# One Trainium2 core, a fused four-layer sequence kernel: a new planner for the order of work in the causal attention stage

## The chip, the core and the metric

The kernel runs on one core of a Trainium2 chip. A core has five engines, each with an instruction queue of its own that is worked off strictly in order: TensorE (PE in the rows; PEld is its weight load), VectorE (DVE), ScalarE (ACT), GpSimd (POOL) and SyncE (SP), which here only issues DMA transfers. They wait for each other through semaphores alone. The metric is the device time of one execution in microseconds (us), a median over runs. TensorE's clock has two levels, 2.4 GHz and 1.2 GHz; the profile gives what was granted as a share of the upper one.

## The reference

Four residual blocks on an input of 4 batches x 1024 rows x 128 features, each behind a layer norm: window attention, gated linear attention, causal attention with a linear recurrence beside it, and a mixture of experts. The change is in the third, which is, cut to what matters:

```python
q, k, v = split_heads(x @ Wqkv_w + Wqkv_b)            # 16 heads of 8
scores = einsum('bhid,bhjd->bhij', q, k) * scale
y_softmax = softmax(scores + causal_mask) @ v
def step(state, inp):                                  # one step per row of the sequence
    q_t, k_t, v_t = inp
    state = retention * state + Gamma * v_t[..., :, None] * (k_t * scale)[..., None, :]
    return state, einsum('bhij,bhj->bhi', W_static + state, q_t)
alpha = sigmoid(gelu(x @ gate_w1 + gate_b1) @ gate_w2 + gate_b2)
y = alpha * y_softmax + (1 - alpha) * y_stp
return y @ out_w + out_b
```

## The kernel before

The causal stage works on 16 units: 4 batches times 4 groups of 4 heads. For each unit it scores twice. The first time (items `M`, 20 to a unit) PE scores 128 query rows against the keys (L1300, with the mask in L1304 and L1307), and DVE takes the negated maximum of each row (L1450, by 512, 768 or 1024 columns). When the maxima of a unit are complete, DVE joins two halves (L1454), POOL splits them into three bf16 parts (L1698 to L1704), PE turns them (item `S`, L1314), ACT copies them out (L1537), and SP moves them into the query stack by four transfers (L1626). The second time (items `W`, 20 to a unit) PE scores keys against queries with the maxima in the stack (L1329, mask L1333 and L1336), ACT takes the exponential into one of four buffers (L1550), and PE weighs the values (items `V`, 12 to a unit, L1357) into an accumulator that ACT copies out (item `A`, L1556). All of `M`, `S`, `W` and the projections and turns below write PE's output into a ring of three PSUM slots of 1024 columns; a slot may be written again when the engine that reads it is through.

Beside the units stands other work. The next batch is prepared: norm (`stats`, `root`, `turn`), the projections `q` and `k` (PE L948, ACT L997 and a bf16 copy L1002; POOL subtracts it, L1669; item `mid` is ACT's second bf16 part, L1006, with POOL's third behind it, L1675; item `write` is SP's transfers of the three parts to a DRAM scratch, L1029; `L` loads them back into the stacks of the batch, L1616, and the batch's first `M` waits for it), and the gate (`gate1`: PE L1260, ACT L1509 between two table loads; `gate2`, `alpha`). ACT's copy L1002 for `k` overwrites the parts of `q`, and so waits until all of `q`'s are in the scratch. The linear recurrence is row work in 8 rounds a batch: `kv` (POOL L1711), `scan` (DVE L1460), `scale` (ACT L1563), `read` (POOL L1723 and L1726, in the first round L1720), and at its end `less` (POOL L1736, 1 minus alpha), `beta` (PE turns it, L1274; ACT L1527 copies it out), `gated` (POOL L1743). A finished batch is turned and projected (`att`: L1368, L1467, L1470, L1479; `tp`: L1376, L1384, L1386, L1488).

`causal_order` writes one list of all items. Every engine's program walks this list and issues its own part of each item, so the list sets each engine's queue. Before the change, the list comes from fixed rules: a `V` stands one key step late, the beside-work stands at hand-given steps (`prepare`, `finish`, 6 steps to a recurrence round), the turned maxima `S` stand behind the second `M` of the next unit, and `M` is put in ahead of `W` by a lead and by a rough estimate of three engines (`TIMES`, `put`, `begin`). The slot of the n-th ring item is n modulo 3:

```python
                    slot[item] = ring[len(slot) % 3]
                    if ps is not None:
                        if len(taken) >= 3:
                            pe_wait_free(taken[-3])
                        taken.append(item)
```

## Time and profile before

| | |
|---|---|
| runs | median 1811.09 us of 3 (1809.95 to 1813.37) |
| the profiled execution | 1810.67 us, its span 1809.4 us |
| causal stage | from 940 to about 1570 us of the span |
| busy in the whole span | PE 1568.5, DVE 1285.6, ACT 1101.3, POOL 698.2 us |
| granted clock, mean | 0.957 |

The median of the runs is 0.42 us above the profiled execution. The sum is made against 1810.67 us. An engine's busy time is what its instructions took; idle time in front of an instruction is put down to the event that ended it. A matmul's end is modelled, so PE's busy time is an upper reading.

### The profile page before, as it was taken

What the parts mean: (1) busy time and instruction counts of PE and PEld (TensorE: products, weight loads), DVE (VectorE), ACT (ScalarE), POOL (GpSimd) and SP (SyncE); (2) the same over time, 40 slices, a digit from 0 to 9 for tenths busy, and PEclk for the clock granted to TensorE, in tenths of its full rate; (3) what the DMA queues carried; (4) which work ended last, traced back from release to release, by engine and by line L of the source; (5) the groups of instructions that cost most, each with busy time, mean ns of one, the idle gap of its engine ahead of it and who ended that gap; (6) DMA issues with size and microseconds to landing.
All of it is one profiled execution on the core that took longest, in us unless ns stands there. A gap on an engine that the chain in (4) does not pass through costs nothing. (4 is left out here: it accounts for less than half of the span.)

```text
span 1809.4 us, 45598 instructions
## 1 busy us (share of the span) xinstructions
PE 1568.5 (87%) x19728; PEld 1003.6 (55%) x19728; DVE 1285.6 (71%) x2035; ACT 1101.3 (61%) x1642; POOL 698.2 (39%) x500
## 2 busy tenths in 40 slices
PE   4577998999999999999977778878888888899999
PEld 2354666778777778777853323433433332566665
DVE  4665745876787687777768768778778886766564
ACT  3265667777777777786733577677677678433321
POOL 4112301544354255425531555556465555301100
PEclk8798998999999999999996989999999999999999
DMA  7864200000000000000142462164236222000000
GB/s 180 198 181 109 41 5 12 2 2 2 1 2 2 2 2 2 2 2 2 48 110 62 146 155 72 48 187 95 71 116 143 72 71 72 1 7 12 7 12 12
DMA packets 43357, 102.59 MB, mean 57 GB/s; under 512 B 3944, under 2 KB 12288, under 8 KB 41428
## 3 DMA queue, kind: packets, MB, share of 16 engines
q1 hardware_dynamic: 40244, 94.17, 20.2%
q10 hardware_dynamic: 2912, 5.51, 1.8%
q8 instruction: 155, 2.54, 0.6%
q14 instruction: 46, 0.38, 0.1%
HBM read 67.42 MB, written 31.46 MB: 55 GB/s over the span
## 5 line engine op out<-in xcount | busy, mean ns | idle before, releaser
L1450 DVE TENSOR_REDUCE arena<-ring 128x2 f32<-128x1024 f32 (+2 forms) x320 | 342.1, 1111 | 88.8 <-PE ring L1307 63.4
L1550 ACT ACTIVATE arena<-ring 128x1024 f32<-128x1024 f32 (+1 forms) x320 | 291.6, 938 | 129.2 <-PE ring L1336 90.2
L1357 PE MATMUL accs<-arena 128*9 128x512 f32 (+3 forms) x1536 | 174.3, 528 | 2.7 <-ACT arena L1550 2.6
L2514 POOL TENSOR_TENSOR arena<-arena 128x1280 f32<-128x1280 f32 x28 | 65.3, 2332 | 287.0 <-PE accs L2275 231.7
L1329 PE MATMUL ring<-arena 51*128 51x512 bf16 (+3 forms) x768 | 124.4, 342 | 46.6 <-DVE arena L1450 24.9
L1300 PE MATMUL ring<-arena 48*128 48x512 bf16 (+3 forms) x768 | 126.6, 342 | 41.9 <-DVE arena L1450 21.7
L2506 POOL TENSOR_TENSOR arena<-arena 128x512 f32<-128x512 f32 x112 | 141.4, 1292 | 3.0 <-DVE arena L2316 3.0
L292 POOL TENSOR_SCALAR xn<-x,moments,rstd 128x128 f32<-128x128 f32 x80 | 64.4, 814 | 198.2 <-DVE rstd L263 182.6
L2781 ACT ACTIVATE arena<-ring 128x512 f32<-128x512 f32 x80 | 47.8, 598 | 147.2 <-PE ring L2636 142.6
L2499 POOL TENSOR_TENSOR arena<-arena 128x1024 f32<-128x1024 f32 x32 | 86.2, 2694 | 108.2 <-DVE arena L2373 108.2
L2741 DVE TENSOR_TENSOR arena<-arena,ring 128x512 f32<-128x512 f32 x80 | 55.0, 688 | 87.8 <-PE ring L2638 74.2
L1723 POOL TENSOR_TENSOR arena<-arena 128x1024 f32<-128x1024 f32 x28 | 65.9, 2355 | 126.6 <-ACT arena L1563 102.5
L1329 PEld LDWEIGHTS ring<-arena 51*128 51x128 bf16 x768 | 36.5, 95 | 140.3 <-DVE arena L1450 78.0
L2658 PEld LDWEIGHTS accs<-weights_large,arena 128*128 128x128 f32 x640 | 83.5, 191 | 27.1 <-issue 23.5
L1300 PEld LDWEIGHTS ring<-arena 48*128 48x128 bf16 x768 | 37.9, 95 | 108.5 <-DVE arena L1450 41.7
L2658 PE MATMUL accs<-weights_large,arena 128*128 128x128 f32 x640 | 84.5, 275 | 0.5 <-DVE arena L2746 0.5
L2459 ACT ACTIVATE arena<-arena 128x512 f32<-128x512 f32 x128 | 81.6, 709 | 0.0
L633 DVE TENSOR_REDUCE arena<-ring 128x8 f32<-128x1024 f32 x49 | 59.3, 1220 | 25.1 <-PE ring L526 25.0
L2251 PE MATMUL ring<-arena 128*64 128x256 f32 x512 | 76.0, 380 | 0.0
L1711 POOL TENSOR_TENSOR arena<-arena 128x1024 f32<-128x1024 f32 x32 | 75.6, 2361 | 0.1
L1460 DVE TENSOR_TENSOR_SCAN arena<-arena 128x1024 f32<-128x1024 f32 x32 | 73.8, 2307 | 2.4 <-POOL arena L1711 2.3
L2316 DVE SCALAR_TENSOR_TENSOR arena<-ring,arena 128x512 f32<-128x512 f32 x32 | 22.1, 692 | 66.6 <-PE ring L2199 66.6
(346 smaller groups left out, 4225.8 us busy)
## 6 DMA issues: line engine op xcount, KB each, us to landing
arena<-whole_k SPq DMA_DIRECT2D x32, 512.0 KB, 4.6
arena<-whole_q SPq DMA_DIRECT2D x32, 512.0 KB, 6.2
arena<-c_scratch_q SPq DMA_DIRECT2D x14, 384.0 KB, 10.2
arena<-c_scratch_k SPq DMA_DIRECT2D x14, 384.0 KB, 13.3
a_scratch_k<-arena SPq DMA_DIRECT2D x8, 512.0 KB
c_scratch_k<-arena SPq DMA_DIRECT2D x8, 512.0 KB, 3.8
arena<-a_scratch_q SPq DMA_DIRECT2D x9, 384.0 KB, 7.2
arena<-a_scratch_k SPq DMA_DIRECT2D x9, 384.0 KB, 9.5
```

The lines of the kernel that those rows point to most:

```text
L1300: mm = nc.tensor.matmul(o[r], qs[half(r, SCORE), pair, n * P:(n + 1) * P], ks[half(r, SCORE), pair, a:c], start=True, stop=not diag)
L1329: mm = nc.tensor.matmul(o[r], ks[half(r, SHIFT), 2 * g + pair, j * P:(j + 1) * P], qs[half(r, SHIFT), 2 * g + pair, a:a + cols], start=Tru ...
L1357: mm = nc.tensor.matmul(acc[ci % 2][32 * h:32 * h + HD + 1, a - c * BANK:BANK], c_values[b % 2][:, j, r * HEADS // 2 + 2 * g + i, :], weig ...
L1450: nc.vector.tensor_reduce(dst, src, AX.X, ALU.max, negate=True).then_inc(c_max_taken.up(item), 1)
L1460: nc.vector.tensor_tensor_scan(sk[:, :], c_retain[:, j:j + 1].to_broadcast([P, T]), sk[:, :], 0.0, ALU.mult, ALU.add).then_inc(c_state_mad ...
L1550: nc.scalar.activation(view(c_probs[wi % 4]), view(ps), ACT.Exp).then_inc(c_weights_made.up(item), 1)
L1711: nc.gpsimd.tensor_tensor(sk[:, :], sk[:, :], c_vT[:, :], ALU.mult).then_inc(c_kv_made.up((b, j)), 1)
L2251: mm = nc.tensor.matmul(ps[r * GLA_D:(r + 1) * GLA_D, o + GLA_D:o + DENSE * GLA_D], k_nat[1][:, cols], v5[t % 2][:, 1:DENSE, cols], start= ...
L2459: nc.scalar.activation(v5[t % 2][:, 1 + r, :], v5[t % 2][:, 0, :], ACT.Copy, scale=route_hot[t // NT % 2][:, t % NT, r:r + 1]).then_inc(v_ ...
L2499: nc.gpsimd.tensor_tensor(masked[0][:, :], masked[0][:, :], masked[1][:, :], ALU.add).then_inc(gla_joined.up(t), 1)
L2506: nc.gpsimd.tensor_tensor(pair_cols(q2m[:, r, :]), pair_cols(q2[t % 2][:, :]), hot_b[t % 2][:, r * P:(r + 1) * P].unsqueeze(1).to_broadcas ...
L2658: mm = nc.tensor.matmul(moe_total[:, n * P:(n + 1) * P], hid[i % 3][:, n * P:(n + 1) * P], w("d_down", f * P, (f + 1) * P), start=f == 0 a ...
```

## The change

`causal_order` gets a new estimate of four engines (PE `P`, ACT `A`, DVE `D`, POOL `G`) with other durations (`STEP`, `NEXT`, `LATER`), a function `ready` that says when an item's data are made by this estimate, and a greedy choice: of `W`, `V`, `S`, `M` and the beside-work on PE, the one that the estimate starts first, with a bonus or malus each. Beside-work without a part on PE goes in where its data are ready by the estimate or three key steps after its due step. `S` is put where the maxima are estimated ready. `less` and the recurrence are two queues, with `after` keeping the order that the data need. A ring item takes the slot that the estimate frees first, and waits for the item that held this slot. The number and kind of instructions stay the same. The core of the diff:

```diff
-            HOP = 0.2
-            TIMES = {"turn": (1.1, (("A", 0.6),), 1), "q": (2.0, (("A", 1.1),), 1), "k": (2.0, (("A", 1.1),), 1),
...
+            HOP, SWITCH = 0.06, 0.2
+            STEP = {"turn": (0.65, ["A", 0.6]), "q": (1.95, ["A", 1.1]), "k": (1.95, ["A", 1.1]), "v": (0.95, ["D", 0.7]),
...
+            LATER = {"root": ["G", 3.3], "turn": ["G", 5.8], "q": ["A", 1.1, "G", 2.2], "k": ["A", 1.1, "G", 2.2],
+                     "mid": ["G", 2.6]}
...
+            def ready(item):
+                kind = item[0]
+                at = lambda *names: max([made.get(n, 0.0) for n in names])
+                if kind == "V":
+                    return at(("W", *item[1:], len(score_pairs(*item[3:5])) - 1))
+                if kind == "W":
+                    return at(("S", *item[1:3], part_of(*item[1:4]))) + (2.2 if item[4:] == (0, 0) else 0.0)
+                if kind == "S":
+                    return at(("neg", *item[1:4]))
...
+                before = {"log": ("stats", b, 3), "root": ("log", b), "gate1": ("turn", b, 1), "gate2": ("gate1", b),
+                          "gate exp": ("gate2", b), "alpha": ("gate exp", b), "less": ("alpha", b), "beta": ("less", b),
+                          "v": ("turn", b, 1), "q": ("turn", b, 1)}
...
+                if kind == "k":
+                    return at(("mid", b, "q", "end")) + 5.0
...
+                return at(before[kind]) if kind in before else 0.0
...
+                if on_ring:
+                    place_of[item] = free.index(min(free))
+                    free[place_of[item]] = done
...
+            def delay(item):
+                pe_time, drain = pe_and_drain(item)
+                behind = clock[drain[0]] - begin(item) - pe_time if drain else 0.0
+                return begin(item) + 0.5 * max(0.0, behind)
+
+            while weights or values or turned:
+                for queue in sides:
+                    while due(queue) and may_go(queue):
+                        put(queue.pop(0)[1])
+                choices = []
+                if weights and not (values and step_of[weights[0][:5]] >= step_of["W", *values[0][1:]] + 2):
+                    if ("S", *weights[0][1:3], part_of(*weights[0][1:4])) in made:
+                        choices.append((delay(weights[0]), "W"))
+                if values and (not weights or step_of[weights[0][:5]] > step_of["W", *values[0][1:]]):
+                    choices.append((begin(values[0]) + (0.25 if weights else 0.0), "V"))
+                if turned and not second:
+                    choices.append((begin(turned[0]) - 0.3, "S"))
...
+                    loaded = not b or ("L", b, "k", g // 2 * 2, g // 2 * 2 + 2) in made
+                    if loaded and taken < (done + most) * ratio and not (turned and last):
+                        choices.append((delay(ahead[0]) - (1.0 if taken < (done + lead) * ratio else 0.0), "M"))
+                if due(sides[0]) and pe_and_drain(sides[0][0][1])[0]:
+                    choices.append((delay(sides[0][0][1]) - 0.2 * (at - sides[0][0][0]), "side"))
+                kind = min(choices)[1]
...
-                    slot[item] = ring[len(slot) % 3]
+                    k = place_of[item] if item in place_of else last_used.index(min(last_used))
+                    slot[item], held_before[item] = ring[k], last_used[k][1]
+                    last_used[k] = len(slot) + 2, item
...
-                    if ps is not None:
-                        if len(taken) >= 3:
-                            pe_wait_free(taken[-3])
-                        taken.append(item)
+                    if held_before.get(item):
+                        pe_wait_free(held_before[item])
```

For an `M` of a later batch the new list asks that its load `L` stands ahead of it (`loaded`); `ready` gives such an `M` no time of its own.

What this moves is shown at three places. Lines are those of each kernel; the new code shifts them by 94 in this stage, so that L1550 becomes L1644, and by 1 in the helpers, so that L997 becomes L998.

ACT, where `k` of the last batch is prepared. Before:

```order
L997 ACTIVATE arena<-ring,arena 128x1024
L1002 ACTIVATE arena<-arena 128x1024
L1563 ACTIVATE arena<-arena,weights_small 128x1024
L1537 ACTIVATE arena<-ring 12x1024
L1550 ACTIVATE arena<-ring 128x1024 x2
L1509 ACT_TABLE_LOAD
L1509 ACTIVATE arena<-ring,weights_small 64x1024
L1511 ACT_TABLE_LOAD
L1550 ACTIVATE arena<-ring 128x1024 x2
L1006 ACTIVATE arena<-arena 128x1024
```

And of the change, with the exponentials ahead of it:

```order
L1007 ACTIVATE arena<-arena 128x1024
L1631 ACTIVATE arena<-ring 12x1024
L1644 ACTIVATE arena<-ring 128x1024 x4
L998 ACTIVATE arena<-ring,arena 128x1024
L1003 ACTIVATE arena<-arena 128x1024
L1605 ACT_TABLE_LOAD
L1007 ACTIVATE arena<-arena 128x1024
L1644 ACTIVATE arena<-ring 128x2x384 x2
```

Between `k`'s first copy and its second part (`mid`) there were four exponentials, a scale and an `S`, and now there is only the gate. The second parts of `q` and `k` are both later in the list. Counted over the list, `k` of batches 1, 2 and 3 stood behind 30, 110 and 190 items `W` and now stands behind 36, 117 and 196; the first `M` of these batches stood behind 46, 126 and 206 and now stands behind 45, 129 and 203. Between `k` and that `M` there were 16 `W` and 20 or 21 `M` each time; now there are 9, 12 and 7 `W` and 12, 12 and 8 `M`.

POOL, the end of the recurrence of the last batch. Before (L1711 is `kv`, L1736 is `less`, L1743 is `gated`):

```order
L1726 TENSOR_TENSOR arena<-arena 128x1024
L1711 TENSOR_TENSOR arena<-arena 128x1024
L1736 TENSOR_SCALAR arena<-arena 128x1024
L1723 TENSOR_TENSOR arena<-arena 128x1024
L1726 TENSOR_TENSOR arena<-arena 128x1024
L1743 TENSOR_TENSOR arena<-arena 128x1024
```

And of the change, where they are L1805, L1830 and L1837:

```order
L1830 TENSOR_SCALAR arena<-arena 128x1024
L1817 TENSOR_TENSOR arena<-arena 128x1024
L1820 TENSOR_TENSOR arena<-arena 128x1024
L1805 TENSOR_TENSOR arena<-arena 128x1024
L1817 TENSOR_TENSOR arena<-arena 128x1024
L1820 TENSOR_TENSOR arena<-arena 128x1024
L1837 TENSOR_TENSOR arena<-arena 128x1024
```

`less` has moved ahead of a `read` (two instructions) and a `kv`; it stands so in all four batches.

PE, at the start of unit (batch 1, group 1), with the slots' numbers. Before:

```order
L1300 MATMUL ring1<-arena 128x512 x2
L1329 MATMUL ring2<-arena 128x512 x2
L1333 MATMUL ring2<-bf_causal_col,bf_half_rows 128x64 x2
L1336 MATMUL ring2<-bf_causal_col,bf_half_rows 128x128 x2
L1300 MATMUL ring0<-arena 128x256 x2
L1304 MATMUL ring0<-bf_causal_row,bf_half_rows 128x128 x2
...
L1329 MATMUL ring1<-arena 128x512 x2
L1333 MATMUL ring1<-bf_causal_col,bf_half_rows 128x64 x2
L1336 MATMUL ring1<-bf_causal_col,bf_half_rows 128x128 x2
L1357 MATMUL accs<-arena 9x128 x4
```

And of the change:

```order
L1451 MATMUL accs<-arena 9x256 x4
L1423 MATMUL ring2<-arena 128x512 x2
L1427 MATMUL ring2<-bf_causal_col,bf_half_rows 128x64 x2
L1430 MATMUL ring2<-bf_causal_col,bf_half_rows 128x128 x2
L1451 MATMUL accs<-arena 9x128 x4
L1423 MATMUL ring1<-arena 128x512 x2
L1427 MATMUL ring1<-bf_causal_col,bf_half_rows 128x64 x2
L1430 MATMUL ring1<-bf_causal_col,bf_half_rows 128x128 x2
L1394 MATMUL ring0<-arena 128x512 x2
L1394 MATMUL ring2<-arena 128x512 x2
L1451 MATMUL accs<-arena 9x512 x4
```

The second `W` of the unit took the slot of the third ring item before it; now it takes that of the second before it. Of the 819 ring items with a holder, 702 keep a distance of three in the new list, 60 have two, 50 have four, and 7 another; alternations of `M` and `W` are about as many as before (an `M` takes a slot from a `W` 158 times before and 155 times now).

## Rows read from the trace of the kernel before

**Rows 1.** Busy time by stretch: us, engines (instructions), granted clock, DMA share, GB/s.

```profile
935.00:1108.00 173.00, 130.44 (x1430) 54.74 (x1430) 134.19 (x147) 94.19 (x109) 73.14 (x57) 0.86 0.50 123
1108.00:1258.00 150.00, 124.42 (x1450) 53.31 (x1448) 117.18 (x133) 103.01 (x121) 83.19 (x54) 0.95 0.42 107
```

**Rows 2.** PE's waits, 940 to 1570 us: in total, times, longest.

```profile
PE ring L1329 <- DVE arena L1450: 24.9, 51, 1.2
PE ring L1300 <- DVE arena L1450: 21.7, 36, 3.1
PE ring L1300 <- ACT arena L1550: 11.6, 29, 1.4
PE ring L1329 <- ACT arena L1537: 9.4, 3, 6.0
PE ring L1314 <- POOL arena L1704: 9.1, 7, 2.1
PE ring L1274 <- POOL arena L1736: 6.7, 4, 3.6
PE ring L1329 <- ACT arena L1550: 5.7, 14, 0.8
```

**Rows 3.** Timeline, 1034 to 1045 us: start, duration, instruction, idle time before it.

```profile
1041.16 1.06 ACT L1002 ACTIVATE arena<-arena 128x1024 bf16<-128x1024 f32 x1 [3.80 <-DMA c_scratch_q<-arena]
...
1044.32 0.61 PE L1329 MATMUL ring<-arena 51*128 51x512 bf16 x2 [6.05 <-ACT arena L1537]
```

**Rows 4.** Timeline at the last batch's `beta`.

```profile
1545.27 1.97 PE L1274 MATMUL ring<-weights_constants,arena 128*128 128x128 f32 x8 [3.60 <-POOL arena L1736]
```

**Rows 5.** Groups by shape, 940 to 1570 us: busy, mean ns, idle before.

```profile
L1450 DVE TENSOR_REDUCE arena<-ring 128x2 f32<-128x1024 f32 x192 | 228.3, 1218 | 52.7 <-PE ring L1307 28.1 <-PE ring L1300 23.4
L1550 ACT ACTIVATE arena<-ring 128x1024 f32<-128x1024 f32 x224 | 222.7, 1023 | 97.9 <-PE ring L1336 60.3 <-PE ring L1329 37.3
L1550 ACT ACTIVATE arena<-ring 128x768 f32<-128x768 f32 x64 | 51.3, 813 | 17.2 <-PE ring L1336 16.2
L1563 ACT ACTIVATE arena<-arena,weights_small 128x1024 f32<-128x1024 f32 x32 | 39.6, 1237 | 5.9 <-DVE arena L1460 5.9
```

**Rows 6.** Timeline of `k` and the gate, batch 2, 1188 to 1202 us.

```profile
1188.49 1.99 PE L948 MATMUL ring<-xnT,weights_small 128*128 128x512 f32 x4
1190.52 1.12 ACT L997 ACTIVATE arena<-ring,arena 128x1024 f32<-128x1024 f32 x1 [3.20 <-PE ring L948]
1191.73 1.06 ACT L1002 ACTIVATE arena<-arena 128x1024 bf16<-128x1024 f32 x1
...
1200.25 1.11 ACT L1509 ACTIVATE arena<-ring,weights_small 64x1024 f32<-64x1024 f32 x1 [1.70 <-PE ring L1260]
...
1201.38 1.28 ACT L1511 ACT_TABLE_LOAD   x1
```

**Rows 7.** Timeline of `mid` and the load of `k`, batch 3.

```profile
1355.75 1.05 ACT L1006 ACTIVATE arena<-arena 128x1024 bf16<-128x1024 f32 x1
...
1361.14 0.77 SPq L1616 DMA_DIRECT2D arena<-c_scratch_k  x2
```

**Rows 8.** L1616 issued 1361.0 to 1361.9 us: time to landing.

```profile
DMA to landing us min/median/max: 8.1/9.0/9.9
```

**Rows 9.** L1616, all of the stage: time to landing.

```profile
DMA to landing us min/median/max: 4.7/10.9/18.3
```

**Rows 10.** L1470 (a line of `att`) and L1454, each one line's instructions.

```profile
L1470 DVE TENSOR_TENSOR arena<-arena x16: 192/194/1905, 1135.1 to 1567.2; 128x32 f32<-128x32 f32 x16
...
L1454 DVE TENSOR_TENSOR arena<-arena x16: 174/176/667, 969.4 to 1510.2; 128x16 f32<-128x16 f32 x16
```

**Rows 11.** Timeline, 1557.9 to 1560.5 us.

```profile
1557.97 2.34 POOL L1743 TENSOR_TENSOR arena<-arena 128x1024 f32<-128x1024 f32 x1
...
1558.46 1.91 DVE L1470 TENSOR_TENSOR arena<-arena 128x32 f32<-128x32 f32 x1
```

More of the change, by code:

```diff
@@ L1 @@
 from contextlib import ExitStack
+from itertools import product
 import numpy as np
@@ L1183, in causal_order @@
-            order += late + [("A", *late[-1][1:4])]
+            second = second[6:]
+            total = len(ahead)
+            weights = [("W", *u, c, j, i) for u in units for c, j in KEY_STEPS for i in range(len(score_pairs(c, j)))]
+            step_of = {("W", *u, *step): k for k, (u, step) in enumerate(product(units, KEY_STEPS))}
+            ratio = total / len(weights) * len(units) / (len(units) - 1)
+            least, most = 9, 19
+            turned = [("S", *units[0], 1)]
+            values, sums, done, at = [], [], 0, -1
@@ new lines, in due, with may_go @@
+            def due(queue):
+                return queue and queue[0][0] <= at and all(i in made for i in after(queue[0][1]))
+            def may_go(queue):
+                first, item = queue[0]
+                pe_time, drain = pe_and_drain(item)
+                return not pe_time and (not drain or at - first >= 3 or ready(item) <= clock[drain[0]] + 0.1)
+            def delay(item):
+                pe_time, drain = pe_and_drain(item)
+                behind = clock[drain[0]] - begin(item) - pe_time if drain else 0.0
+                return begin(item) + 0.5 * max(0.0, behind)
@@ L1185, in causal_order @@
+            for _, item in sides[1] + sides[0]:
+                put(item)
             end, rows = finish(batches - 1), moe_order()
@@ L1242, in pe_program @@
             def pe_program():
-                taken = []
                 pe.wait_ge(weights_in[s], "all")
```

176 lines of the change are left out of this document (105 added, 71 removed), and 11 rows, old and new, of tables (STEP, TIMES).

## The prediction

> **What bounds the kernel now.** I read the stretches of the span first. The change touches only the causal stage, 630 of 1809.4 us. A middle batch takes 150 us (batch 2 and batch 3 read alike, one row stands), and in it no engine is full: PE is busy 124.4 us (83%), DVE 117.2 (78%), ACT 103.0 (69%) and POOL 83.2 (55%) [rows 1]. So the stage is bound by the order in which PE, DVE and ACT hand ring slots to each other, and a new order can gain: at most PE's 25 us of idle time in such a batch, near 100 us in the stage. The first batch takes 173 us, PE idle for 43 of them and its clock at 0.86 [rows 1]; the new list changes little at its start, and I count nothing there but the one stall below. A perfect order would still leave some of it, since only three slots feed two engines that take 1.218 us for a maximum and 1.023 us for an exponential [rows 5].
>
> PE's waits say what ends that idle time [rows 2]. A slot that DVE (L1450) or ACT (L1550) has yet to read costs 24.9 + 21.7 + 11.6 + 5.7 = 63.9 us. The turned maxima waiting for POOL (L1704) cost 9.1, `beta` waiting for `less` (L1736) 6.7, and a `W` waiting for the copy of an `S` (L1537) 9.4. The last is mostly one stall of 6.05 us at 1044.32 [rows 3], and the row above it tells its cause: ACT stood 3.80 us in front of its copy of `k` until the scratch transfers of `q` were through, with the `S` copy behind it in its queue, and PE stood behind that.
>
> **The change part by part.** No instruction is added or removed, so every term is a wait. The sum is made against the profiled execution, 1810.67 us, 0.42 below the median of the runs.
>
> *`k` later, batch 1.* Between `q`'s `mid` and `k` there were 4 `W` and 2 `M`; now there are 4 `W` and 7 `M`. Five more maxima at 1.218 us [rows 5] are 6.1 us, more than the 3.80 us that ACT stood. I take the whole stall: **-6** (bounds 0 and -6.05). In batches 2 and 3 no such stall stands in the trace, and the distance grows too.
>
> *`less` ahead of a `read` and a `kv`.* POOL ran `less` behind them, and in the last batch PE stood 3.60 us for it [rows 4]. Now it runs while POOL waits for a `scale`. The four waits are 6.7 us; what is late next is `scan` and `scale` of the last round, but `gated`, which ends at 1560.31 [rows 11], is needed only by the second projection of finished rows, and even 2 us later it stays beside the next stage's first blocks. I take **-6** (bounds 0 and -6.7).
>
> *`S` where its maxima are ready.* Mostly five to eight items of the list now stand between a unit's last `M` and its `S`, against four to eight, some of them one `M` only. I take two thirds of 9.1: **-6** (bounds 0 and -9.1).
>
> *Slots and the choice between `M`, `W` and `V`.* This is the widest term. The slot rule by itself changes 117 of 819 places, and the kinds alternate as often as before; the list is rearranged rather than regrouped. What can go is the time in which PE stands before a slot whose drain engine is late while another slot is free, or in which it feeds the busier of DVE and ACT. I take a quarter of 63.9: **-16**. The lower bound is 0; the upper is 40, because a third of the waits at least is the ring's own, a maximum's 1.218 us lying open wherever PE has nothing else. A loss here would need the estimate to mistake which engine is late; its durations (1.215 us for 512 columns twice, 1.02 for the exponential) are those of the rows, so I exclude more than 5 us of it.
>
> *The load of the next batch's stacks comes later than its first `M` wants it.* This one is a new wait. From PE's start of `k`, the chain is: 2.0 us until ACT starts (1188.49 to 1190.52), 1.12 + 1.06 on ACT with a gap, ending at 4.3 [rows 6]; then the gate, now directly behind it on ACT: 1.28 + 1.11 + 1.28, the first table load as long as the second [rows 6], ending at 8.0; then `mid` to the issue of the load of `k`, 1355.75 to 1361.14 = 5.4 [rows 7], to 13.4; then the landing, 9.9 [rows 8], to **23.3 us**. Before, 16 `W` and 20 `M` (34 us at the middle batches' 150 us for 80 pairs, 1.87 us each) stood in that gap. Now batch 3 has 7 `W` and 8 `M`. ACT, the busier engine there, needs 2.0 + 2.2 + 3.7 + 1.05 for `k`, gate and `mid`, 2 x 0.813 + 4 x 1.023 and about 0.5 (half a full one) for the seven exponentials, and 1.24 for a scale [rows 5]: 16.4 us, with a copy and a small exponential some 17.5. The `M` waits 5.8 us, with PE's whole queue behind it, `W` and `V` among them, and so DVE and ACT too. Batch 1 has nine exponentials, 19.5 us, and waits 3.8; batch 2 has twelve, some 22.6 us and more `V` than the others, and hardly waits. Sum **+10** (bounds 0 and, with the longest landing of the stage, 18.3 in place of 9.9 [rows 9], +35).
>
> *A burst on ACT.* Without an exponential between `k` and its `mid`, ACT's copies and the gate take 7 us in a row. The slots of `k` and `gate1` were held just as long before, and DVE can go on with `M` from the third. I take 0 (bounds 0 and +5).
>
> *POOL against DVE.* At 1558.46 a DVE product with 32 columns took 1.91 us while POOL's L1743 ran [rows 11]; the same line has a median of 194 ns, and L1454 176 ns with a longest of 667 [rows 10]. The new list changes which DVE operations meet a POOL one, at random as far as I see: 0, with bounds of two such meetings more or fewer, 1.7 us each, -4 and +4. The Trainium skill, "SBUF — State Buffer", section "SBUF: two separate sides", has this as a rule: a DVE operation with two SBUF inputs and a GpSimd operation hold the shared ports exclusively, and the later one blocks for the whole instruction. By this rule, the trace agrees, and the new estimate, which lets both engines run at once, would promise more than the chip gives; it would take a few us from the gain and not its sign.
>
> Sum: -6 - 6 - 6 - 16 + 10 = -24, and 1810.67 - 24 = 1786.7. I predict **1786 us**.
>
> **The rivals.**
> 1. *The forecast: a gain of 12 to 40 us* (1771 to 1799), chance 0.52.
> 2. *The slot waits mostly go*, a gain over 40 us. For it: PE's idle time is 25 us a batch and its waits are short (51 and 36 times, longest 1.2 and 3.1 us) [rows 2], which better alternation removes. Against it: three slots stay three slots. With the 16 at 40 the sum is 1763. Chance 0.14.
> 3. *Nothing that matters*: the stage's waits change place. The terms for `k`, `less` and `S` are then eaten by the load, and the slots give 2 or 3 us: 1810.67 - 18 + 10 - 3 = 1800, or up to 1820 if the burst and the ports take their bounds. For it: alternation as before, DVE already at 78%. Chance 0.16.
> 4. *Slower: PE waits for the stacks in each batch.* The load of `k` competes on the DMA queues with the fetches of the recurrence, and its landing goes to the 18.3 us seen at the longest [rows 9]: 8.4 us more in each of three batches, so +35 in place of +10, and the slot term gives nothing: 1810.67 - 18 + 35 = 1828. It decides from a landing some 6 us longer than 9.9 on, with the slot term at 0. A faster pace makes it worse, since the chain of 23.3 us doesn't shrink with the items that cover it. Chance 0.18.
>
> **How the numbers follow.** A difference of 0.2%, 3.6 us, is about what a measurement of this kernel can tell from none. Faster by more than that: all of 1 and 2, half of 3: 0.74. Within it: 0.07. Slower: 4 and a little of 3: 0.19. The range holds 8 in 10: down to 1764, which takes in most of case 2, and up to 1812, which takes in most of case 3 and leaves case 4 out.
>
> **What would show each step.** Right: a middle batch takes 142 to 147 us in place of 150, with DVE busy 80% or more; no wait of ACT for the scratch of `q` near the first batch's end; L1274's successor no longer waits for POOL; the successor of L1300 waits for the load of `k` (a DMA) some 3 to 6 us in front of batches 1 and 3; and the waits for L1450's and L1550's successors fall by about 16 us from 63.9. Everything outside the stage keeps its time. The prediction would be wrong if these slot waits fall by half or don't fall, or if a wait for a load exceeds 10 us; and if POOL's turned maxima come later than now because a `read` stands ahead of them in its queue.

## The result and the profile after

The changed kernel takes **1831.50 us** (median of 4 runs, 1827.71 to 1833.28) against 1810.62 us for the kernel before on the same chip, a ratio of 1.011 [1.009, 1.0129]: 1.1% slower, where 1.4% faster was forecast, and outside the range of 1764 to 1812. Its profiled execution took 1831.15 us.

The causal stage first, from the start of its first maximum to that of its last accumulator copy, in each kernel's own window; the columns are those of [rows 1]. Before:

```profile
940.65:1553.97 613.32, 496.58 (x5713) 209.55 (x5710) 478.50 (x548) 401.07 (x468) 314.40 (x216) 0.93 0.40 99
```

and after, with its first stretch and the two behind it, which are, near enough, the second and third batch:

```profile
943.53:1574.25 630.72, 508.76 (x5705) 222.16 (x5702) 488.77 (x547) 402.60 (x466) 311.92 (x215) 0.91 0.39 97
...
935.00:1106.00 171.00, 136.51 (x1389) 60.23 (x1389) 132.84 (x145) 91.73 (x104) 64.05 (x53) 0.81 0.49 119
1106.00:1263.00 157.00, 128.08 (x1474) 57.87 (x1470) 125.13 (x137) 107.90 (x124) 89.08 (x60) 0.94 0.44 109
1263.00:1420.00 157.00, 125.73 (x1444) 55.98 (x1446) 121.60 (x134) 100.90 (x116) 77.48 (x53) 0.94 0.39 96
```

The stage is 17.4 us longer (630.72 against 613.32). PE's busy time in it grew by 12.2 us (508.76 against 496.58) though it holds the same instructions (5705 records against 5713); its idle time, what is left of the window, grew by only 5.2 (121.96 against 116.74). The mean granted clock fell from 0.93 to 0.91, most of all in the first stretch, 0.81 against 0.86 [rows 1]. Summed over the trace's records of the grant, PE stood at the lower level, 1.2 GHz, for 119.5 us of the stage, before for 88.7. A matmul record takes longer there: in the changed kernel's stage the median of a `W` matmul of 512 columns is 606 ns there and 386 ns at 2.4 GHz, that of a `V` matmul of 512 columns 1057 and 593. PE was busy at the lower level for 103.5 us, before for 75.2. The 28.3 us between, shortened by these two ratios, give 10.3 to 12.4 us (an estimate), and that is the 12.2. It isn't the chance of one execution either: over its four executions the changed kernel was granted 0.9465 in the mean, the kernel before 0.953 to 0.955 on each of five chips. Everything behind the stage takes what it took, 255.6 us against 255.4; the remaining 2.9 us of the 20.5 lie ahead of the first maximum, which the change doesn't touch; that start lay between 936.7 and 952.3 us over the kernels measured below.

PE's waits in the stage, as in [rows 2]:

```profile
PE ring L1394 <- DVE arena L1544: 20.5, 32, 3.1
PE accs L1451 <- ACT arena L1644: 20.2, 33, 1.1
PE ring L1423 <- DVE arena L1544: 19.6, 36, 3.1
PE ring L1394 <- ACT arena L1644: 15.9, 41, 0.9
PE ring L1394 <- DMA arena<-c_scratch_k: 10.9, 3, 7.4
PE ring L1408 <- POOL arena L1798: 8.5, 7, 2.4
PE ring L1423 <- ACT arena L1644: 7.3, 12, 3.6
...
PE ring L1394 <- ACT arena L1631: 1.9, 4, 0.5
```

The four slot rows, L1394 and L1423 behind L1544 and L1644, make 20.5 + 15.9 + 19.6 + 7.3 = 63.3 us against 63.9: unmoved. The copy of an `S` (L1631) is down from 9.4 to 1.9, and a wait of `beta` for `less` is no longer there at all. Two waits are new: a `V` behind its exponential, 20.2 us in 33 pieces (2.6 before), and the load.

The load, on ACT, SP's queue and PE, batch 3:

```profile
1362.97 1.11 ACT L998 ACTIVATE arena<-ring,arena 128x1024 f32<-128x1024 f32 x1 [1.98 <-PE ring L949]
1364.18 1.06 ACT L1003 ACTIVATE arena<-arena 128x1024 bf16<-128x1024 f32 x1
1365.25 1.28 ACT L1603 ACT_TABLE_LOAD   x1
1366.55 1.11 ACT L1603 ACTIVATE arena<-ring,weights_small 64x1024 f32<-64x1024 f32 x1
1367.67 1.28 ACT L1605 ACT_TABLE_LOAD   x1
1368.97 1.06 ACT L1007 ACTIVATE arena<-arena 128x1024 bf16<-128x1024 f32 x1
...
1375.13 0.77 SPq L1710 DMA_DIRECT2D arena<-c_scratch_k  x2
...
1385.78 0.29 PE L1394 MATMUL ring<-arena 48*128 48x128 bf16 x2 [7.38 <-DMA arena<-c_scratch_k]
```

The burst on ACT is there as drawn: `k`, its copy, the gate between two table loads and `mid` follow each other within 7.1 us (1362.97 to 1370.03). The load goes out at 1375.13, PE's `M` starts 10.7 us later, and PE has stood for 7.38.

### The profile page after: what moved, and what is told of

Its sections match the earlier page's. It is cut to its first block and busy times, and to the rows that moved or that the text cites. A ratio compares the mean times of both kernels' runs of the same rounds, so it can differ in the third digit from the quotient of the medians.

```text
span 1829.8 us, 45578 instructions
## 1 busy us (share of the span) xinstructions
PE 1581.4 (86%) x19728; PEld 1017.9 (56%) x19728; DVE 1296.0 (71%) x2035; ACT 1102.1 (60%) x1642; POOL 696.6 (38%) x500
## 3 DMA queue, kind: packets, MB, share of 16 engines
q1 hardware_dynamic: 40244, 94.17, 20.2%
## 5 line engine op out<-in xcount | busy, mean ns | idle before, releaser
L1544 DVE TENSOR_REDUCE arena<-ring 128x2 f32<-128x1024 f32 (+2 forms) x320 | 345.7, 1111 | 93.7 <-PE ring L1401 50.1
L1644 ACT ACTIVATE arena<-ring 128x1024 f32<-128x1024 f32 (+1 forms) x320 | 290.9, 938 | 160.7 <-PE ring L1430 91.2
L1451 PE MATMUL accs<-arena 128*9 128x512 f32 (+3 forms) x1536 | 175.3, 531 | 20.6 <-ACT arena L1644 20.2
L1394 PE MATMUL ring<-arena 48*128 48x512 bf16 (+3 forms) x768 | 131.2, 351 | 56.7 <-DVE arena L1544 20.5
L1423 PE MATMUL ring<-arena 51*128 51x512 bf16 (+3 forms) x768 | 127.0, 348 | 29.9 <-DVE arena L1544 19.6
L293 POOL TENSOR_SCALAR xn<-x,moments,rstd 128x128 f32<-128x128 f32 x80 | 67.4, 856 | 211.1 <-DVE rstd L264 207.6
L1394 PEld LDWEIGHTS ring<-arena 48*128 48x128 bf16 x768 | 38.6, 97 | 136.8 <-issue 46.5
L1423 PEld LDWEIGHTS ring<-arena 51*128 51x128 bf16 x768 | 37.6, 95 | 132.5 <-issue 64.3
L1554 DVE TENSOR_TENSOR_SCAN arena<-arena 128x1024 f32<-128x1024 f32 x32 | 79.3, 2479 | 11.9 <-POOL arena L1805 11.8
L1805 POOL TENSOR_TENSOR arena<-arena 128x1024 f32<-128x1024 f32 x32 | 75.5, 2360 | 0.1
L2343 PEld LDWEIGHTS ring<-arena 128*64 128x64 f32 x512 | 36.1, 135 | 60.3 <-issue 30.6
## 6 DMA issues: line engine op xcount, KB each, us to landing
arena<-c_scratch_q SPq DMA_DIRECT2D x14, 384.0 KB, 10.7
```

What stands on the lines that cost most here:

```text
L293: nc.gpsimd.tensor_scalar(xn[n % 4][:, :], x[:, b * NT + n, :], moments[:, n, 0:1], rstd[:, 3, n:n + 1], ALU.subtract, ALU.mult).then_inc( ...
L1394: mm = nc.tensor.matmul(o[r], qs[half(r, SCORE), pair, n * P:(n + 1) * P], ks[half(r, SCORE), pair, a:c], start=True, stop=not diag)
L1423: mm = nc.tensor.matmul(o[r], ks[half(r, SHIFT), 2 * g + pair, j * P:(j + 1) * P], qs[half(r, SHIFT), 2 * g + pair, a:a + cols], start=Tru ...
L1451: mm = nc.tensor.matmul(acc[ci % 2][32 * h:32 * h + HD + 1, a - c * BANK:BANK], c_values[b % 2][:, j, r * HEADS // 2 + 2 * g + i, :], weig ...
L1544: nc.vector.tensor_reduce(dst, src, AX.X, ALU.max, negate=True).then_inc(c_max_taken.up(item), 1)
L1554: nc.vector.tensor_tensor_scan(sk[:, :], c_retain[:, j:j + 1].to_broadcast([P, T]), sk[:, :], 0.0, ALU.mult, ALU.add).then_inc(c_state_mad ...
```

## The experiments

Each list was run as a kernel of its own. The table gives for each its median, the ratio to the kernel before on the same chip, PE's time at 1.2 GHz in the stage, and PE's busy and idle time there, taken as above; the first two lines are the kernels of the case. The runs are spread over several chips, so times of different lists are compared by their ratios. The last three columns are of one execution each, the profiled one, and are rougher than the medians: e18, whose list differs from the changed one by a single swap of two neighbours, has 10.3 us less at 1.2 GHz. What lies ahead of the stage varies too, though no edit touches it: in e11 PE was at 1.2 GHz for 99.0 us there, before for 68.3, and 11.6 of the 28.5 us by which its profiled execution is longer lie there.

| list | us | ratio | 1.2 GHz | busy | idle |
|---|---|---|---|---|---|
| before | 1810.6 | | 88.7 | 496.6 | 116.7 |
| changed | 1831.5 | 1.011 [1.009, 1.0129] | 119.5 | 508.8 | 121.9 |
| e4 before, `less` first | 1809.3 | 0.9975 [0.9961, 0.9989] | 93.4 | 499.0 | 111.8 |
| e13 before, pause 0.15 | 1815.5 | 1.0025 [1.0014, 1.0037] | 113.3 | 505.7 | 113.0 |
| e15 before, maximum +3% | 1814.2 | 1.002 [1.0009, 1.0032] | 95.6 | 499.4 | 117.4 |
| e2 each `V` one later | 1831.4 | 1.0098 [1.0071, 1.0125] | 126.3 | 514.0 | 119.8 |
| e3 slots in turn | 1834.0 | 1.0115 [1.0083, 1.0147] | 133.1 | 512.7 | 123.3 |
| e9 load earlier, last batch | 1830.2 | 1.0114 [1.009, 1.0138] | 112.6 | 508.0 | 121.4 |
| e6 chain of `q`, `k` earlier | 1834.0 | 1.0128 [1.0103, 1.0154] | 126.3 | 503.7 | 132.6 |
| e1 load known | 1814.3 | 1.0002 [0.9982, 1.0022] | 92.2 | 500.5 | 113.6 |
| e5 load known, last batch | 1811.9 | 1.0005 [0.9988, 1.0022] | 99.0 | 503.3 | 111.2 |
| e8 e1, row work with margin | 1822.7 | 1.0071 [1.0038, 1.0104] | 116.1 | 510.5 | 110.2 |
| e7 weight 0.4 | 1813.3 | 1.0005 [0.9987, 1.0024] | 95.6 | 499.8 | 110.8 |
| e11 weight 0.45 | 1835.7 | 1.0134 [1.0105, 1.0164] | 139.9 | 513.9 | 116.1 |
| e16 weight 0.55 | 1813.2 | 1.002 [1.0001, 1.0039] | 109.2 | 504.2 | 109.0 |
| e12 weight 0.6 | 1830.0 | 1.0116 [1.0094, 1.0137] | 102.4 | 497.9 | 130.5 |
| e17 malus of `V` 0.2 | 1829.6 | 1.0107 [1.0081, 1.0134] | 139.9 | 517.0 | 117.0 |
| e18 bonus of `S` 0.2 | 1828.3 | 1.009 [1.0062, 1.0119] | 109.2 | 505.5 | 123.6 |
| e10 weight 0.4, load known | 1801.8 | 0.9953 [0.9929, 0.9978] | 95.6 | 499.1 | 100.7 |
| e19 weight 0.45, load known | 1827.9 | 1.0083 [1.0053, 1.0113] | 119.5 | 506.5 | 117.4 |

**e4: `less` alone, in the list of before.**

```diff
-                side[end + 6].append(("less", b))
+                side[end + 6].insert(0, ("less", b))
```

> The kernel before, with less alone put ahead of the read and kv of its step. If the term of 6 us for it was sized right: PE's waits for L1736 go from 6.7 to near 0 and the time is 0.996 to 0.998 of the kernel before. If the wait is only passed on (POOL's recurrence is 1 us later, PE stands before another slot): 0.999 to 1.000.

The wait of 6.7 us is gone and the kernel gains 0.25%, 4.6 us. The term of the prediction holds nearly whole.

**e1 and e5: the planner knows when a load lands**, in all batches and in the last alone.

```diff
+                if kind == "M" and item[1]:         # e5: item[1] == 3
+                    return at(("mid", item[1], "k", "end")) + (11.6 if item[2] < 2 else 17.6)
```

> The changed kernel, whose estimate now also knows when the stacks of the next batch land (second part of k done + 11.6 us, + 17.6 for the second half of the groups). Theory L (the load stands in front of the first M): PE's waits for the load of k fall from 10.9 to under 3 us and the time falls by 6 to 9 us against the changed kernel, to 1.006 to 1.008 of the kernel before. Theory V (most of the loss is that a V stands too close behind its exponential): at most 3 us are gained, since PE then waits for an exponential in place of the load. Theory S (the slot rule costs it): no change, 1.011.

> The changed kernel with the landing of the stacks known to the estimate for the last batch only; the list is the changed one up to that point. The same rule for all batches brought 20 us. Theory L1 (the one wait of 7.4 us for the load of the last batch, and what it drags behind it to the end, is the loss): 1.000 to 1.004 of the kernel before, batch 3 of the stage (between the ends of the second and third batch) near 150 us in place of 159. Theory L2 (all loads count, and batch 2 loses for other reasons): 1.006 or more.

Both come out level with the kernel before. In e1 the load's wait in the last batch is 1.1 us in place of 7.4, in e5 none. But by the ratios 19 to 20 us came back in both for a wait of 8.4 (the 10.9 above less the very first load, 2.5, which stands ahead of the first maximum), and PE's time at 1.2 GHz fell with it from 119.5 to 92.2 and 99.0 us. So the rule brought back more than the wait it was written for, and what else it changed was still open.

**e9: the load earlier, nothing else**, by moving the last batch's `mid` and `write` of `q` 16 items and `k`, `gate1`, `mid` and `write` of `k` 12 items ahead in the changed list.

```diff
+            earlier([("mid", 3, "q"), ("write", 3, "q")], 16)
+            earlier([("k", 3), ("gate1", 3), ("mid", 3, "k"), ("write", 3, "k")], 12)
```

> The changed kernel's own list with a hand edit at one place: mid and write of q of the last batch 16 items earlier, k, gate1, mid and write of k 12 items earlier, so that 11 W in place of 7 stand between the write of k and the first M of that batch. All else stays. Theory L (the wait for the load is the largest single part of the loss): the wait of 7.4 us falls under 1.5 us, unit (2, 2) takes 29 to 31 us in place of 37.6, and the time falls by 6 to 10 us, to 1.005 to 1.008 of the kernel before. If the wait was covering other waits: under 4 us gained. If it is the whole cause: 1.000 to 1.003.

The load's wait is gone but for the very first, and the kernel is as slow as the changed one. Its waits in the stage:

```profile
PE ring L1403 <- DVE arena L1553: 23.6, 31, 3.8
PE accs L1460 <- ACT arena L1653: 20.2, 34, 1.1
PE ring L1403 <- ACT arena L1653: 18.4, 40, 2.6
...
PE ring L1432 <- ACT arena L1653: 11.6, 13, 4.3
...
PE ring L1403 <- DMA arena<-c_scratch_k: 2.2, 1, 2.2
```

L1403 and L1432 are the L1394 and L1423 of the changed kernel. Their waits for ACT (L1653) went from 15.9 + 7.3 to 18.4 + 11.6, the longest to 4.3. The unit in which the load had been awaited shrank from 37.6 to 29.4 us, and the one ahead of it, where ACT's work on `k` now stands, grew from 47.4 to 58.8 (from one unit's last accumulator copy to the next unit's). PE's idle time is the same to 0.5 us. The timeline of ACT and PE in the longer unit tells what came in the load's place:

```profile
1336.57 1.06 ACT L1007 ACTIVATE arena<-arena 128x1024 bf16<-128x1024 f32 x1 [3.95 <-POOL arena L1772]
...
1338.60 0.61 PE L1432 MATMUL ring<-arena 51*128 51x512 bf16 x2 [4.31 <-ACT arena L1653]
...
1358.14 0.23 PE L1403 MATMUL ring<-arena 48*128 48x128 bf16 x2 [1.30 <-ACT arena L1612]
...
1361.42 0.61 PE L1403 MATMUL ring<-arena 48*128 48x512 bf16 x2 [2.60 <-ACT arena L1653]
```

The first pair is made by the edit itself: with `mid` of `q` 16 items ahead, one `W` stands between `q` and its `mid` where seven stood, so ACT stands 3.95 us for POOL's subtraction (L1772) and PE 4.31 us behind ACT. The changed kernel has no such wait. The other two, 3.90 us, come behind ACT's burst on `k`. So e9 doesn't give the price of the load's wait by itself: 7.4 us went and 8.2 came, of which 4.3 by the early `mid`.

**e2: every `V` swapped with the score behind it.**

```diff
+            for i in range(len(order) - 2, 0, -1):
+                if order[i][0] == "V" and order[i + 1][0] in "MW":
+                    order[i], order[i + 1] = order[i + 1], order[i]
```

> The changed kernel with every V moved behind the M or W that follows it in the list, nothing else. Theory V: PE's waits in front of L1451 for the exponential fall from 20.2 to under 6 us and the time falls by 10 to 17 us, to 1.002 to 1.006 of the kernel before. Theory L: at most 4 us, the load's wait of 10.9 stays. Theory S: no change. A rival to V: the wait only moves to the slots (the M or W that now goes first stands for its slot), which shows as more than 63 us there and an unchanged time.

Nothing gained. The waits of e2, whose lines are shifted by 3:

```profile
PE ring L1426 <- DVE arena L1547: 25.8, 46, 3.2
PE ring L1397 <- DVE arena L1547: 23.0, 42, 3.1
PE ring L1426 <- ACT arena L1647: 15.6, 27, 4.8
...
PE accs L1454 <- ACT arena L1647: 2.6, 7, 0.6
```

The `V`'s 20.2 us are 2.6, and the slots behind DVE and ACT took them: 25.8 + 23.0 + 15.6 alone are more than the 63.3 of all four, which are now 75.2. So 11.9 of the 17.6 us came back at the slots; idle time in all fell by 2.2 us, and busy time grew by 5.3. Most of a wait behind an exponential is no loss of its own; it is the same wait for a drain engine (ACT or DVE, which read PE's output), at another instruction.

**e3: the changed list with slots in turn.**

```diff
-                    k = place_of[item] if item in place_of else last_used.index(min(last_used))
+                    k = len(slot) % 3
```

> The changed kernel's list with the three slots in turn, as before the change. Theory S (the slot rule costs time, since its releases are estimated): faster than the changed kernel by 5 us or more. Theories L and V: the rule has little part in it; slower by 0 to 6 us, 1.011 to 1.015 of the kernel before.

The ratio is 1.0115 against the changed kernel's 1.011, well inside the two intervals: the slot rule is worth little and is not the loss.

**e6: the chain of `q` and `k` due earlier**, with `mid` and `write` of `k` left at their steps.

```diff
-                7: [("root", b)], 10: [("turn", b, 0)], 12: [("turn", b, 1)], 13: [("q", b)], 14: [("v", b, 0)],
-                15: [("mid", b, "q")], 16: [("write", b, "q"), ("v", b, 1)], 17: [("k", b)], 18: [("gate1", b)],
+                7: [("root", b)], 8: [("turn", b, 0)], 9: [("turn", b, 1), ("q", b)], 10: [("mid", b, "q"), ("write", b, "q")],
+                11: [("v", b, 0)], 12: [("v", b, 1)], 13: [("k", b)], 18: [("gate1", b)],
```

> The changed kernel with turn, q, mid, write and k due 2 to 5 steps earlier, so that 13 W in place of 7 to 12 cover the load of k. The load rule of the estimate stays unaware. Theory L: the waits for the load of k fall under 4 us, and the time comes to 1.000 to 1.005, by another edit than the first. If the first edit only found a better list by luck, this one should stay at 1.008 or more. If k stalls ACT again for the scratch of q, the row of L1003 shows it.

Waits for a load now stand in all three batches, 6.4, 5.2 and 6.6 us. Between PE's `k` and the first `M` stand 13 `W`, more than the 9, 12 and 7 of the changed kernel, but between `write` of `k` and that `M` only 7 in each batch, where the changed kernel has 9, 12 and 7 (waits 0, 1.0 and 7.4). So the distance from the scratch write counts, not that from `k`. e12 has 10, 5 and 5 and waits 14.5 us in two batches. The slower time of e6 is not the loads' alone, though: its edit puts `mid` of `q` directly behind `q`, and ACT stood 17.9 us in front of it for POOL's subtraction, in three pieces of up to 7.1 us, where the changed kernel has none.

**e8: e1 with the recurrence's scans and scales only when they are ready by a margin.**

```diff
-                return not pe_time and (not drain or at - first >= 3 or ready(item) <= clock[drain[0]] + 0.1)
+                return not pe_time and (not drain or at - first >= (5 if item[0] in ("scan", "scale") else 3)
+                                        or ready(item) <= clock[drain[0]] - (0.9 if item[0] in ("scan", "scale") else -0.1))
```

> The changed kernel with the landing known, and scan and scale put in only when their data have been ready for 0.9 us by the estimate (or five steps late). In the changed kernel DVE stood 11.8 us in front of scans for kv and ACT 6.3 us in front of scales. Theory R (row work placed without a margin holds up ACT and DVE): these waits fall under 6 us together and the time is 3 to 8 us under that of the first experiment, 0.996 to 0.999. Rival: the recurrence ends later and the stage's end waits for gated: slower than the first experiment by 2 to 6 us.

0.7% slower than before, and slower than e1. The edit did what it was for: DVE stood 9.7 us in front of scans, in e1 17.0. PE's idle time is 3.4 us less than e1's, its busy time 9.9 more, with 23.9 us more at 1.2 GHz; and the work behind the stage took 261.6 us in place of 255.6, with 6.8 us at 1.2 GHz and a wait of 2.0 us for the copy of `beta` (L1624), which e1 doesn't have there.

**e7, e11, e16, e12: one neutral number**, the weight of a late drain engine (0.5 in the changed kernel), and **e17, e18**, two others of the same kind.

```diff
-                return begin(item) + 0.5 * max(0.0, behind)
+                return begin(item) + 0.4 * max(0.0, behind)        # e11 0.45, e16 0.55, e12 0.6
...
-                choices.append((begin(values[0]) + (0.25 if weights else 0.0), "V"))
+                choices.append((begin(values[0]) + (0.2 if weights else 0.0), "V"))      # e17
...
-                    choices.append((begin(turned[0]) - 0.3, "S"))
+                    choices.append((begin(turned[0]) - 0.2, "S"))      # e18
```

> The changed kernel with the weight of a drain engine's backlog at 0.4 in place of 0.5: as neutral a change of the greedy choice as I can make, to see how much any change of the list moves the time. k and the first M of the last batch are 9 W apart in place of 7. Theory L: the time falls by 0 to 5 us, as the load's wait falls by about 2 to 4 us. If lists differ by chance by more than the effects that I name: a time over 8 us from the changed kernel's, either way.

> The changed kernel with the backlog weight at 0.45; the load is unknown to the estimate. 11 W stand between the write of k and the first M in all three batches. Theory L: waits for the load under 1.5 us each, 1.000 to 1.004 of the kernel before. If what decides is chance in the list, it can stand anywhere from 0.998 to 1.012.

> The changed kernel with the backlog weight at 0.6. 10, 5 and 5 W stand between the write of k and the first M. Theory L: waits for the load near 0 to 2, 9 and 9 us, and 1.010 to 1.018 of the kernel before. If chance in the list decides, it can as well be at 1.00, waits or not.

> The changed kernel, its weight of a late drain 0.55 in place of 0.5. 0.4, 0.45, 0.5 and 0.6 gave 1813.3, 1835.7, 1831.5 and 1830.0. Theory A (scatter): anywhere from 1805 to 1835 us, and the half-clock time in the stage goes with it. Theory B (weights from 0.45 on are worse by their rule): 1828 to 1836 us.

> The changed kernel, the malus of a weighing of the values 0.2 in place of 0.25: it comes a little earlier against the scores. Theory A (scatter): anywhere from 1805 to 1835 us. Theory B (weighings directly behind their exponentials are what costs): 1832 to 1840 us, with the waits of the weighings behind their exponentials over 20.2 us.

> The changed kernel, the bonus of an S 0.2 in place of 0.3: one single place of TensorE's queue differs, two maxima against a neighbour in one unit. Theory A (the falls of the granted clock hang on the exact places of waits, so that even this moves the stage): more than 5 us from the changed kernel's 1831.5. Theory B (a list's time is set by its larger shape, and such a swap is lost): 1828 to 1835 us, half-clock time in the stage near 119.5 us.

Five weights give 1813.3, 1835.7, 1831.5, 1813.2 and 1830.0 us, ratios of 1.0005, 1.0134, 1.011, 1.002 and 1.0116. No trend: these lists are near the kernel before or over 1% slower, by a number that means nothing. e18, in which one `S` stands one `M` later, stays at 1828.3, so the theory that any swap can tip the list fell there. The two ways to be slow come apart in two of these lists. Their stages:

```profile
936.65:1570.67 634.02, 517.03 (x5705) 223.58 (x5702) 482.66 (x547) 403.24 (x467) 313.59 (x215) 0.89 0.39 96
```

is e17, and e12 is

```profile
941.83:1570.28 628.45, 497.93 (x5705) 217.82 (x5702) 486.38 (x547) 402.95 (x466) 305.22 (x215) 0.92 0.39 97
```

e17 has the idle time of before (116.99 against 116.74) and its stage is 20.7 us longer by busy time alone, at a clock of 0.89; PE was busy at 1.2 GHz for 127.1 us of it, before for 75.2. e12 has the busy time of before within 1.4 us and is slower by 13.8 us of idle time, with 14.5 us of waits for loads. The fast ones differ from the slow by idle time too: e16 was granted 0.9467 in the mean of its ten executions, no more than the changed kernel's 0.9465, and is 1% faster with 13.0 us less idle time in the stage.

**e13 and e15: neutral numbers in the planner of before.**

```diff
-            HOP = 0.2
+            HOP = 0.15                                             # e13
...
-                    return 0.00077 * per * (c - a) + mask, (("D", 0.16 + 0.00204 * per * (c - a)),), 1
+                    return 0.00077 * per * (c - a) + mask, (("D", 0.16 + 0.0021 * per * (c - a)),), 1      # e15
```

> The kernel before, its planner's pause between engines 0.15 us in place of 0.2: few rows move, by chance. Theory A (any list of about this kind lands within some 12 us of another by where waits and half-clock stretches fall, whatever rule made it): lists of before scatter too, this one anywhere from 1800 to 1825 us. Theory B (the lists of before are steady and the changed planner's rules are worse): 1809 to 1814 us, half-clock time in the stage near the 88.9 us of before.

> The kernel before, its planner's duration of a maximum 3% longer: a larger rearrangement of the rows of maxima by a neutral number. Theory A (scatter of lists of any planner): 1800 to 1830 us. Theory B (before is steady, the new rules are worse): 1809 to 1816 us.

Both are a little slower, +0.25% and +0.2%. Four lists of the old rules lie within 0.5% by the ratios, 0.9975 to 1.0025, and within 0.25% without e4, which takes a wait away. But its beside-work is fixed by hand, so these lists differ less from each other than those of the new rules do: 103 (e13) and 567 (e15) of the 1382 places of the list hold another item than before, and 662 to 968 in e7, e11, e12, e16 and e17 against the changed list. And the clock moves under the old rules as well: e13 has 113.3 us at 1.2 GHz, nearly the 119.5 of the changed kernel, and 9.1 us more busy time than before. Its idle time is 3.8 us less.

**e10 and e19: a weight and the known load together**, the edits of e7 and of e11 with that of e1.

> Backlog weight 0.4 (which alone gave 1.0005 with waits of 3.2, 0.3 and 2.0 us for the loads) and the landing known to the estimate. Theory L: these 5.5 us go, 0.996 to 0.999. If a new list brings other waits of its own by chance: 1.000 to 1.006.

> Weight 0.45 with the estimate knowing when the loads land; 0.45 without it gave 1835.7 us and no wait for a load in batches 1 to 3, but 139.9 us at the half clock. Theory A (the rule helps by taking load waits away): none to take, 1830 to 1838 us. Theory B (the rule keeps more scores between, spreads the beside-work and so TensorE's busy time, and the clock falls less often): 1802 to 1818 us with under 105 us at the half clock. Theory C (scatter): anywhere between 1800 and 1838 us.

e10 takes **1801.84 us**, 0.9953 [0.9929, 0.9978], and **beats both kernels**: 0.5% faster than the kernel before, with 16.0 us less idle time in the stage than the kernel before and 2.5 more busy time. e19 has no wait for a load to lose either with the rule or without it, and its ratio is 0.5% lower with it: in the stage of the profiled executions busy time fell by 7.4 us, idle time rose by 1.3. It stays slow. So the rule seems to act on more than the load's wait, but doesn't decide the time; one pair of lists shows no more.

## What the clock does in this stage

Stretches of e17, columns as in [rows 1], around its longest time at the lower level:

```profile
1354.90:1358.40 3.50, 3.50 (x28) 0.92 (x28) 0.69 (x1) 3.38 (x3) 1.15 (x1) 1.00 1.03 253
1358.40:1361.80 3.40, 1.46 (x24) 0.68 (x20) 3.33 (x3) 3.36 (x4) 0.98 (x1) 0.99 0.85 334
1361.80:1365.20 3.40, 3.14 (x32) 1.24 (x34) 3.40 (x3) 2.70 (x4) 2.13 (x1) 0.50 0.48 177
1365.20:1368.60 3.40, 3.40 (x28) 3.40 (x25) 1.12 (x1) 0.60 (x1) 0.00 (x0) 0.50 1.05 243
1368.60:1372.00 3.40, 3.40 (x32) 1.20 (x31) 1.87 (x3) 0.84 (x1) 0.00 (x0) 0.50 1.08 174
```

In the second row DVE and ACT work without a gap (3.33 and 3.36 of 3.40) and PE, which waits for the slots that they hold, is busy for 1.46. Behind it the clock is at 0.50, 1.2 GHz, and stays there to 1382.2. Two rows on, PE is busy all the time and DVE and ACT stand (1.12 and 0.60): PE, which was ahead of its drain engines, is now the one that both wait for. A cluster of waits so costs twice here, once as idle time and once as slow matmuls behind it; that the waits bring the fall of the clock is read from the order of the rows and not shown by an experiment. The Trainium skill, "TensorE: Matmul & The Clock Gate", section "A second HAM failure mode: psum-queue depth-cycling", tells of small idles between groups of matmuls, made by cycling PSUM banks, that let the clock swing. The trace agrees in that the clock falls behind such idles at PSUM slots; how often they bring a fall is not shown.

The load wait of the changed kernel does it as well:

```profile
1378.60:1382.00 3.40, 0.00 (x0) 0.00 (x0) 0.61 (x2) 0.65 (x1) 2.38 (x5) 1.00 0.99 154
1382.00:1385.40 3.40, 0.00 (x0) 0.00 (x0) 0.00 (x0) 0.00 (x0) 3.32 (x3) 0.50 1.11 183
1385.40:1388.80 3.40, 3.02 (x38) 1.80 (x39) 1.74 (x2) 0.81 (x1) 2.25 (x1) 0.50 1.00 154
```

The clock falls while PE stands and is low for 6.8 us, in which PE works for 3.0. That is little: 6.8 of the 30.7 us more at the lower level, and some 1.1 of the 12.2 us of busy time (an estimate, by the 606 and 386 ns above).

Over the twenty lists of the table busy time follows the time at 1.2 GHz with a correlation of 0.91 and 0.34 us of busy time for each us at that level. For the changed kernel's 30.7 us that gives 10.6 of the 12.2.

## Why the prediction was wrong

It summed waits and left the length of the matmuls alone; and the largest of its waits, the slots, didn't move. Point by point:

- *`k` later, -6*: right in mechanism and in kind. The copy of an `S` fell from 9.4 to 1.9 us, and no wait for the scratch of `q` is left on PE's path.
- *`less`, -6*: right. The wait of 6.7 is gone; alone it is worth 4.6 us (e4).
- *`S` turned, -6*: wrong. 9.1 became 8.5 (L1408), and was between 4.2 and 18.4 in the other lists of the new rules: where the estimate is a us off, the wait stays.
- *Slots and the choice, -16*: **the failed step**. "I take a quarter of 63.9" had no row behind it: 63.3 stand there. The `V`s, drawn closer to their exponentials, took 17.6 us more besides, and e2 shows most of these to be of the same stock. The prediction said that a loss would need the estimate to mistake which engine is late, and excluded more than 5 us. DVE shows where it can: the estimate has a scan at 2.3 us and POOL beside it at will, and the scans took

```profile
L1554 DVE TENSOR_TENSOR_SCAN arena<-arena 128x1024 f32<-128x1024 f32 x32 | 79.3, 2479 | 11.9 <-POOL arena L1805 11.8
```

against, before,

```profile
L1460 DVE TENSOR_TENSOR_SCAN arena<-arena 128x1024 f32<-128x1024 f32 x32 | 73.8, 2307 | 2.4 <-POOL arena L1711 2.3
```

so 5.5 us more in themselves and 9.5 more standing at the head of DVE's queue, with the maxima behind them. That this keeps the gain away is not shown, and the lists speak against it: DVE stood 20.0 us in front of scans in e10, the fastest, and 19.5 in e7, and e8, which cut it to 9.7, isn't faster. Why the slot waits stay at 63.3 is open.
- *The load, +10*: right, 8.4 us measured. The size by batch was 0, 1.0 and 7.4 where 3.8, 0 and 5.8 were said. What it costs by itself stays open, since e9 takes it away and puts 8.2 us of other waits in its place.
- *The burst and the ports, 0*: the burst is there, and PE doesn't wait for ACT between 1362.97 and 1370.03; in e9 3.9 us of PE's waits follow the same burst. The ports cost DVE the 5.5 us above.
- *Not in the sum*: the granted clock. With the idle waits at +5.2 us where the sum had -24, and busy time at +12.2 where it had 0, the stage's 17.4 us are told. By what PE stood for, the +5.2 are: ACT's exponentials +16.8 (27.6 to 44.4), the load +8.4, the copies of `S` -7.0, `less` -6.7, all else -6.3. The clock was in [rows 1] with 0.86 in the first stretch, and I read it as a property of the start, not as something that a list can move.

Of the rivals the fourth named nearly the time, 1828, but not the way: no landing is late by 6 us in each batch, and one batch waits, not three. The third, whose waits change place, fits the idle time of the stage, and has no clock in it. The check named in the prediction, a middle batch of 142 to 147 us, came out at 153.4 and 159.2.

What stays open: which property of a list sets off the clusters. Lists of the new rules with the load unknown are fast in 2 and slow in 5 of 7 of this kind (weights and the two others), and nothing that I counted in them (waits for loads, for exponentials, for slots, DVE's for scans) sorts the two groups. PE's busy and idle time do, but these two are the stage itself. In e16 the time at 1.2 GHz is high (109.2) and the idle time low (109.0), and it is fast. Whether a clock held up by force would bring back the busy time was not tried.

## What to carry to other kernels

This greedy planner, whose estimate knows one speed of TensorE, gives lists that scatter by 1% for numbers without meaning, so one list says little about a rule: run a handful with neighbouring numbers, and keep the best (here e10, 0.5% faster than the kernel before). Split a stage's change into busy and idle time of the bounding engine before explaining it: the same instructions with more busy time point to the clock, and no wait will account for them. And where a wait is removed, look at the sum of idle time, not at its row: in e2 most of a wait changed its name, and in e9 and e6 the edit that was to take a wait away made a new one, ACT standing for POOL.

## What the hardware showed that I had not expected

The scan with two inputs in SBUF beside a POOL product, in the changed kernel:

```profile
1182.46 2.14 POOL L1763 TENSOR_TENSOR arena<-arena 128x1024 f32<-128x1024 f32 x1
1182.54 4.21 DVE L1554 TENSOR_TENSOR_SCAN arena<-arena 128x1024 f32<-128x1024 f32 x1 [0.67 <-POOL arena L1805]
```

It was issued 0.08 us behind POOL's instruction and took 4.21 us, where the scans of before have a mean of 2.307. 4.21 is the 2.06 left of POOL's 2.14 and 2.15 of its own. Eight scans of the changed kernel were lengthened in this way, all issued while a POOL instruction ran: they took 2.38 to 4.21 us and ended 2.15 us behind the end of POOL's (1.79 behind L293), where the median scan takes 2.28. Together they are 6.4 us over that, in the kernel before two scans are 0.9 over it; the 5.5 us above are between. The Trainium skill, "SBUF — State Buffer", section "SBUF: two separate sides", has the rule that the later of two such instructions waits for the whole of the other; the trace agrees. I had put a meeting at 1.7 us and left its sum at 0; this one cost 1.9.

The clock also goes with the time from run to run of one kernel: over the 129 executions of e1 to e12 and of the kernel before beside them, each against the mean of its own kernel and chip, 0.01 less of the mean granted clock goes with 9.2 us more (correlation 0.67). And in the kernel before the stretches at 1.2 GHz come again from batch to batch, at 1185.1 and 1335.3, 1195.4 and 1345.6, 1219.3 and 1369.4: 150.2 us apart, as the batches are. Chance would not place them so: at least these are set by the list.
